# The order of the steps on five queues of a decoder block, written anew

## The chip, the cores and the metric

The kernel runs on one core of one Trainium2 chip. The metric is the device time in microseconds (us), the median of three runs. The profile comes from one execution of its own. Engines in the profile: PE is TensorE, PEld its weight loads, DVE is VectorE, ACT is ScalarE, POOL is GpSimd, SPq the sync queue, which here issues all transfers.

## The reference

One decoder block for 32 batches of 256 tokens with 256 features, in float32. Each of the three parts works on a LayerNorm of x and is added to x:

```
x = x + attn(layernorm(x))          # a: 8 heads of 128, one shared K and V, causal softmax, Wo
x = x + xattn(layernorm(x), ctx)    # b: 16 heads of 16 on a context of 256 tokens;
                                    #    scores get two bias tensors (one of 32x16x256x256) and a padding mask
x = x + ffn(layernorm(x))           # c: shared expert 0 and 8 experts of 256, relu squared,
                                    #    gate: top 2 of 8, sigmoid, normalized
```

## The kernel before

Matmuls are done in float16 pairs (a high and a low part of each operand, three products), so each tile has a `hi` and a `lo` that engines other than TensorE make. Each of the five queues (sync, GpSimd, ScalarE, VectorE, TensorE) has a list of steps, written out by hand in `ORDERS`. An entry `b_s:5@4` is step `b_s` for head 5 of the batch 4 iterations back. `iterations` walks each list 32 + 6 times and emits the steps whose batch exists. So the three parts run at once on different batches: in the loop part a is some two batches ahead of part c. A queue works strictly in its list's order; steps wait for each other through semaphores that count, and the same name on several engines is one step's share on each.

The steps that matter here, with their lines:

- `b_load:p` (sync, L363 to L368) loads the bias of a pair of heads, 512 KB, into one of four slots, once VectorE has read the slot (`b_s` of head 2p+1). `b_pT:j` (sync, L421) transposes head j's probabilities by DMA. `b_store_q`, `b_store_k` write q and k to DRAM (L388, L381), `b_stack_q`, `b_stack_k` read them back stacked, 8 loads each (L413, L402). `b_s:0` on TensorE waits for all 16.
- `b_s:j`: scores on TensorE (L1088, two matmuls, which wait until VectorE has done head j-1), bias and maximum on VectorE (L828), exponential on ScalarE (L662, L664, which waits for VectorE's `b_p` of head j-1). `b_p:j`: probabilities, high part on ScalarE (L672), low part on VectorE (L835). `b_pv:j` on TensorE (L1102). `b_comb:j` (GpSimd, L520) adds the mask to the bias.
- `b_mask` (VectorE, L814) makes the mask of a batch; `b_ln`, `b_T`, `b_q`, `b_kv`, `b_o`, `b_wo` are LayerNorm, its transposition, the projections and the output of part b.
- `a_wo` is part a's output projection, 48 matmuls; `a_kv` and `a_q:r` its projections (TensorE's `a_q:0` waits for VectorE's `a_kv`, L758), `a_s:h`, `a_pt:h`, `a_pv:h` scores, transposition and values of head h.
- `c_ln`, `c_T` (L992, then ScalarE L582 and VectorE L743) give part c its input. `c_gate` on TensorE are 16 small matmuls; on VectorE `c_gate:0` to `c_gate:12` are 13 steps on 8 or 16 columns, of which `c_gate:4` (L890) waits for ScalarE's exponential (L684), `c_gate:5` casts (L893), `c_gate:6` makes masks (L898). `c_f1:e` is expert e's first matmul (TensorE L965), relu (ScalarE L690) and square (GpSimd L534), `c_sq:e` the high part of the square (ScalarE L695), `c_lo:e` the low part (GpSimd L541). `c_f2:e` is the second matmul and, on VectorE, the sum into `acc` (L936); TensorE's `c_f2:e` waits for VectorE's `c_f2:e-1`, and VectorE's `c_f2:1` for the last gate step.
- `w_split:n` (ScalarE and VectorE) splits a piece of the weights, in the first batch alone.

TensorE's waits in two of these steps read:

```
            def b_s(b, j):
                if j == 0:
                    pe.wait_ge(b_qst_ok, after(b, STACK, STACK))
                    pe.wait_ge(b_kst_ok, after(b, STACK, STACK))
                pe.wait_ge(b_t_ok, after(b, BH, j))
...
            def c_f2(b, e):
                pe.wait_ge(c_h_ok, after(b, NX, e + 1))
                if e == 0:
                    pe.wait_ge(c_gd, after(b, GATE_STEPS, 1))
                else:
                    pe.wait_ge(c_a_ok, after(b, NX, e))
```

Of the kernel before, what the change touches and what calls it, by code (L numbers as in the profile page):

```python
# [66 lines left out]
def order(text):  # L67
# [9 lines left out]
        b_pT:11@5 b_load:5@5 b_pT:13@5 b_load:7@5 b_store_q:0@4 b_pT:14@5 b_store_k:0@4 b_pT:15@5 b_stack_q:0@4  # L77
        b_stack_k:0@4 a_T:0@3 b_load:6@5 b_load:0@4 b_pT:0@4 b_load:1@4 b_pT:1@4 c_f2:8@6 b_pT:2@4 b_pT:3@4
        b_pT:4@4 b_load:2@4 b_pT:5@4 b_pT:6@4 b_mask:0@4 b_split_q:0@3 b_load:3@4 a_ln:0@3 b_pT:8@4 b_pT:7@4
        b_pT:9@4 b_pT:10@4 b_load:4@4 b_pT:12@4""",  # L80
    gpsimd="""
        b_comb:9@5 b_comb:10@5 b_comb:11@5 c_lo:4@6 c_f1:5@6 c_lo:5@6 c_f1:6@6 b_comb:12@5 a_ln:0@3 b_ln:0@4
        b_comb:13@5 b_comb:14@5 a_kv:0@3 b_comb:15@5 c_lo:6@6 a_q:0@3 b_split_q:0@4 c_f1:7@6 c_lo:7@6
        b_split_k:0@4 a_q:1@3 b_comb:0@4 a_q:2@3 c_f1:8@6 c_lo:8@6 a_q:3@3 b_comb:1@4 b_kv:0@3 b_comb:2@4
        c_ln:0@5 b_comb:3@4 b_v:0@4 b_comb:4@4 b_comb:5@4 c_f1:0@5 c_lo:0@5 b_comb:6@4 c_f1:1@5 b_comb:7@4
        c_lo:1@5 c_f1:2@5 c_lo:2@5 b_res:0@4 c_f1:3@5 c_lo:3@5 b_comb:8@4 c_f1:4@5""",
    scalar="""
        a_n:3@2 a_pt:2@2 a_pv:1@2 a_s:6@2 a_n:4@2 b_s:0@3 c_ln:0@4 b_p:0@3 a_pt:3@2 c_T:0@4 a_pv:2@2 b_s:1@3
        b_p:1@3 a_n:5@2 a_pt:4@2 b_s:2@3 c_f1:0@4 b_p:2@3 c_gate:0@4 c_sq:0@4 a_s:7@2 c_f1:1@4 b_s:3@3 a_pv:3@2
        w_split:9@2 b_p:3@3 c_f1:2@4 a_pt:5@2 c_sq:1@4 b_s:4@3 c_f1:3@4 b_p:4@3 w_split:10@2 c_sq:2@4  # L90
        w_split:11@2 a_n:6@2 c_f1:4@4 b_s:5@3 b_p:5@3 a_pv:4@2 c_sq:3@4 a_pt:6@2 b_s:6@3 b_p:6@3 c_f1:5@4
        a_n:7@2 b_s:7@3 a_pv:5@2 b_p:7@3 c_sq:4@4 w_split:12@2 c_f1:6@4 b_s:8@3 a_pv:6@2 a_pt:7@2 b_p:8@3
        c_sq:5@4 w_split:13@2 w_split:14@2 w_split:15@2 a_pv:7@2 b_s:9@3 b_p:9@3 c_f1:7@4 b_s:10@3 b_p:10@3
# [1135 lines left out]
```

## Time and profile before

| | |
|---|---|
| median of 3 runs | 2400.63 us (2398.98 to 2402.5) |
| the profiled execution | 2400.63 us, its span 2398.8 us |
| mean granted TensorE clock | 0.954 |
| busy shares | PE 89%, ACT 87%, DVE 83%, POOL 74% |
| chain that ended last | PE 48%, DVE 21%, issue 14%, ACT 13% |
| transfers | 367 MB, 153 GB/s, 70.7% of the 16 DMA engines' time |

Busy shares are of the span. The chain is followed back from the last instruction; "issue" in it, and as the releaser of a wait, is time for which no engine's work is the cause that the profile shows. The clock is the share of full speed (2.4 GHz) that TensorE was granted; 0.50 is 1.2 GHz. The span from batch to batch is called an interval below, from one start of `b_wo` on TensorE to the next.

### The profile page before, as it was taken

The numbers are of one execution on the slowest core, as the hardware profiler recorded it, in microseconds if no ns is written. First come the engines' busy times: TensorE is split into PE (matmuls) and PEld (weight loads), VectorE is DVE, ScalarE is ACT, GpSimd is POOL, SyncE is SP. The second block draws the span as 40 slices with busy tenths as digits, with TensorE's granted clock in tenths as the row PEclk, the third lists the DMA queues.
The fourth block names the chain that finished last, engine by engine and source line by source line (L and its number), as shares of the span: only waits on it lengthen the run. The fifth ranks groups of instructions, "written<-read, shape, count | busy, mean of one in ns | idle before, by whom it ended". The sixth has DMA issues, their size and how long they took to land.

```text
span 2398.8 us, 73036 instructions
## 1 busy us (share of the span) xinstructions
PE 2130.8 (89%) x24128; PEld 1855.2 (77%) x24128; DVE 1987.0 (83%) x6672; ACT 2079.4 (87%) x6065; POOL 1786.7 (74%) x1899
## 2 busy tenths in 40 slices
PE   4679999999999999998999999999999988999876
PEld 3468888888877878887778888888888877788755
DVE  5478889888888888888888888899888888888763
ACT  5589999988988999998999999999998889899862
POOL 2448788877877877877877878787778777777773
PEclk9789999999999999999999999999999999999987
DMA  4377766768767788877867777677678678878760
GB/s 148 113 173 155 168 146 162 171 153 160 159 155 142 173 157 158 162 155 138 169 155 164 161 157 163 145 174 160 161 163 156 150 147 158 162 160 157 142 145 22
DMA packets 711784, 367.16 MB, mean 153 GB/s; under 512 B 561392, under 2 KB 659952, under 8 KB 711408
## 3 DMA queue, kind: packets, MB, share of 16 engines
q1 hardware_dynamic: 711408, 362.50, 70.7%
q8 instruction: 193, 3.16, 0.6%
q14 instruction: 183, 1.50, 0.2%
HBM read 202.98 MB, written 25.17 MB: 95 GB/s over the span
## 4 chain that ended last, share of the span: by engine, by line
PE 48%; DVE 21%; issue 14%; ACT 13%; POOL 2%; DMA 2%; SPq 0%; DVEq 0%; ACTq 0%; POOLq 0%
PE ps_a_misc L965 13%; PE ps_c_hidden L965 10%; PE ps_c_out L965 9%; PE ps_a_scores L1025 4%; DVE b_neg_scores L828 3%; DVE g_mask L898 2%; PE ps_b_misc L1102 2%; PE ps_b_scores L1088 2%; ACT ps_b_probs L664 2%; PE ps_a_misc L1044 2%; DVE b_probs_hi_lo L835 2%; ACT ps_b_probs L662 2%; ACT b_probs_hi_lo L672 2%; DVE g_weights L920 1%; DVE g_sum L913 1%
## 5 line engine op out<-in xcount | busy, mean ns | idle before, releaser
L520 POOL TENSOR_TENSOR bias<-bias,b_mask 128x512 f32<-128x512 f32 x512 | 646.4, 1274 | 7.2 <-DMA bias<-in_bias 7.0
L835 DVE TENSOR_TENSOR b_probs_hi_lo<-ps_b_probs,b_probs_hi_lo 128x512 f16<-128x512 f32 x512 | 351.8, 687 | 128.9 <-ACT b_probs_hi_lo L672 127.3
L828 DVE CUSTOM_DVE_ANT_0 b_neg_scores<-ps_b_scores,bias 128x256 f32<-128x256 f32 x1024 | 389.3, 417 | 72.0 <-PE ps_b_scores L1088 60.4
L534 POOL TENSOR_TENSOR c_hidden<-c_relu 128x512 f32<-128x512 f32 x288 | 299.8, 1041 | 152.7 <-ACT c_relu L690 138.0
L541 POOL TENSOR_TENSOR c_hidden_lo<-c_hidden,c_hidden_hi 128x512 f16<-128x512 f32 x288 | 334.2, 1160 | 59.8 <-issue 39.4
L662 ACT ACTIVATE ps_b_probs<-b_neg_scores,b_neg_max 128x256 f32<-128x256 f32 x512 | 245.4, 479 | 144.0 <-DVE b_probs_hi_lo L835 108.7
L965 PE MATMUL ps_c_hidden<-c_xT_hi,w_hi 128*128 128x256 f16 x1152 | 325.1, 282 | 40.1 <-ACT c_relu L690 40.0
L965 PE MATMUL ps_c_out<-w_hi,c_hidden_hi 128*128 128x256 f16 x1152 | 316.1, 274 | 29.0 <-DVE acc L936 28.9
L965 PE MATMUL ps_c_hidden<-c_xT_lo,w_hi 128*128 128x256 f16 x1152 | 324.0, 281 | 0.0
L965 PE MATMUL ps_c_hidden<-c_xT_hi,w_lo 128*128 128x256 f16 x1152 | 323.6, 281 | 0.0
L965 PE MATMUL ps_c_out<-w_hi,c_hidden_lo 128*128 128x256 f16 x1152 | 316.3, 275 | 0.0
L965 PE MATMUL ps_c_out<-w_lo,c_hidden_hi 128*128 128x256 f16 x1152 | 316.2, 274 | 0.0
L672 ACT ACTIVATE b_probs_hi_lo<-ps_b_probs 128x512 f16<-128x512 f32 x512 | 303.1, 592 | 8.4
L936 DVE SCALAR_TENSOR_TENSOR acc<-ps_c_out,g_weights,acc 128x256 f32<-128x256 f32 x512 | 218.6, 468 | 29.6 <-PE ps_c_out L965 29.6
L664 ACT ACTIVATE ps_b_probs<-b_neg_scores,b_neg_max 128x256 f32<-128x256 f32 x512 | 239.9, 469 | 0.0
L1102 PE MATMUL ps_b_misc<-b_v_hi,b_probsT_hi_lo 128*128 128x16 f16 x4096 | 217.1, 170 | 5.6 <-DMA b_probsT_hi_lo<-b_probs_hi_lo 5.5
L1102 PEld LDWEIGHTS ps_b_misc<-b_v_hi,b_probsT_hi_lo 128*128 128x128 f16 x4096 | 203.2, 96 | 11.5 <-DMA b_probsT_hi_lo<-b_probs_hi_lo 7.0
L478 POOL TENSOR_TENSOR a_qT_lo<-a_qT,a_qT_hi 128x512 f16<-128x512 f32 x128 | 148.8, 1162 | 78.6 <-ACT a_qT_hi L601 74.7
L690 ACT ACTIVATE c_relu<-ps_c_hidden 128x512 f32<-128x512 f32 x288 | 169.9, 590 | 31.3 <-PE ps_c_hidden L965 27.7
L1102 PE MATMUL ps_b_misc<-b_v_lo,b_probsT_hi_lo 128*128 128x16 f16 x2048 | 194.1, 169 | 0.0
L695 ACT ACTIVATE c_hidden_hi<-c_relu 128x512 f16<-128x512 f32 x288 | 181.9, 632 | 5.8 <-PE ps_c_out L965 5.8
L965 PE MATMUL ps_a_misc<-a_xT_hi,w_hi 128*128 128x256 f16 x576 | 159.4, 277 | 13.3 <-DVE a_v_lo L758 8.8
(194 smaller groups left out, 7752.5 us busy)
## 6 DMA issues: line engine op xcount, KB each, us to landing
bias<-in_bias SPq DMA_DIRECT2D x256, 512.0 KB, 4.1
q_stack<-qk_scratch SPq DMA_DIRECT2D x256, 64.0 KB, 3.6
x_ln<-in_x SPq DMA_DIRECT2D x32, 256.0 KB, 3.1
ctxT<-in_ctx SPq DMA_DIRECT2D x32, 256.0 KB, 2.8
x<-in_x SPq DMA_DIRECT2D x32, 256.0 KB, 4.0
qk_scratch<-b_qT_hi_lo SPq DMA_DIRECT2D x32, 256.0 KB, 5.5
qk_scratch<-b_kT_hi_lo SPq DMA_DIRECT2D x32, 256.0 KB, 4.2
k_stack_even<-qk_scratch SPq DMA_DIRECT2D x128, 64.0 KB, 2.9
```

The source lines that it names most:

```text
L520: gp.tensor_tensor(part, part, b_mask[:, :], ALU.add).then_inc(b_c_ok, 1)
L534: gp.tensor_tensor(c_h[:, :], c_r[:, e % 2, :], c_r[:, e % 2, :], ALU.mult).then_inc(c_sq_ok, 1)
L541: gp.tensor_tensor(c_hl[:, u, :], c_h[:, :], c_hh[:, u, :], ALU.subtract).then_inc(c_h_ok, 1)
L662: act.activation(ps_bp[:, 0:T], b_t[:, u, 0, :], ACT.Exp, bias=b_mx[:, u, 0:1], scale=-1.0, accum_out=b_sum[:, 0, j:j + 1])
L664: act.activation(ps_bp[:, T:2 * T], b_t[:, u, 1, :], ACT.Exp, bias=b_mx[:, u, 1:2], scale=-1.0, accum_out=b_sum[:, 1, j:j + 1]).then_inc(b ...
L672: act.activation(b_p2[:, j % DEPTH, :, 0, :], ps_bp[:, :].rearrange("p (c t) -> p c t", c=CT), ACT.Copy).then_inc(b_ph_ok, 1)
L695: act.activation(c_hh[:, e % 2, :], c_r[:, e % 2, :], ACT.Square).then_inc(c_hh_ok, 1)
L828: last = dve.tensor_tensor_reduce(out=b_t[:, u, c, :], in0=ps_bs[:, c * T:(c + 1) * T], in1=bias[:, slot, at:at + T], scale=-2.0, scalar=3 ...
L835: dve.tensor_tensor(b_p2[:, j % DEPTH, :, 1, :], ps_bp[:, :].rearrange("p (c t) -> p c t", c=CT), b_p2[:, j % DEPTH, :, 0, :], ALU.subtrac ...
L936: last = dve.scalar_tensor_tensor(out=acc[:, c, :], in0=ps_c2[:, c * D:(c + 1) * D], scalar=g_we[:, c, e - 1:e], in1=acc[:, c, :], op0=ALU ...
L965: last = pe.matmul(out, stat(s, k), mov(m, k), start=(k == 0 and n == 0), stop=(k == chunks - 1 and n == len(parts) - 1))
L1102: last = pe.matmul(ps_bm[:, at:at + BD], b_pT[:, u, c, part, s, :], v[:, s, j * BD:(j + 1) * BD], start=(s == 0 and n == 0), stop=(s == CT ...
```

## The change

All five lists in `ORDERS` are replaced. Each has the same steps as before, once each, so the instructions, their shapes and their number stay; what changes is the place of a step in its queue and with it what it waits behind. Where a list begins is of no weight by itself (a list that starts one step later has its lags written differently), only the order in the endless round counts. `w_split` entries count for the first batch alone. The lines of the old and the new lists that the text speaks of:

```diff
     sync="""
-        b_pT:11@5 b_load:5@5 b_pT:13@5 b_load:7@5 b_store_q:0@4 b_pT:14@5 b_store_k:0@4 b_pT:15@5 b_stack_q:0@4
-        b_stack_k:0@4 a_T:0@3 b_load:6@5 b_load:0@4 b_pT:0@4 b_load:1@4 b_pT:1@4 c_f2:8@6 b_pT:2@4 b_pT:3@4
-        b_pT:4@4 b_load:2@4 b_pT:5@4 b_pT:6@4 b_mask:0@4 b_split_q:0@3 b_load:3@4 a_ln:0@3 b_pT:8@4 b_pT:7@4
-        b_pT:9@4 b_pT:10@4 b_load:4@4 b_pT:12@4""",
+        b_load:7@5 b_store_q:0@4 b_pT:14@5 b_mask:0@4 b_store_k:0@4 b_pT:15@5 b_stack_q:0@4 b_stack_k:0@4
+        c_f2:8@6 b_load:0@4 b_pT:0@4 b_pT:1@4 b_load:1@4 a_ln:0@3 a_T:0@3 b_pT:2@4 b_pT:3@4 b_pT:4@4 b_load:3@4
+        b_load:2@4 b_pT:5@4 b_pT:7@4 b_pT:6@4 b_load:4@4 b_pT:8@4 b_split_q:0@3 b_load:5@4 b_pT:9@4 b_pT:10@4
+        b_pT:11@4 b_load:6@4 b_pT:12@4 b_pT:13@4""",
     gpsimd="""
...
-        c_ln:0@5 b_comb:3@4 b_v:0@4 b_comb:4@4 b_comb:5@4 c_f1:0@5 c_lo:0@5 b_comb:6@4 c_f1:1@5 b_comb:7@4
-        c_lo:1@5 c_f1:2@5 c_lo:2@5 b_res:0@4 c_f1:3@5 c_lo:3@5 b_comb:8@4 c_f1:4@5""",
+        b_v:0@4 b_comb:5@4 a_q:3@3 b_comb:6@4 c_ln:0@5 b_res:0@4 c_f1:0@5 c_lo:0@5 c_f1:1@5 c_lo:1@5 b_kv:0@3
+        c_f1:2@5 c_lo:2@5 b_comb:7@4 c_f1:3@5 b_comb:8@4 c_lo:3@5 b_comb:9@4 c_f1:4@5 c_lo:4@5 c_f1:5@5 c_lo:5@5
+        b_comb:10@4 b_comb:11@4 c_f1:6@5 b_comb:12@4 a_ln:0@2 c_lo:6@5 b_comb:13@4 b_ln:0@3 b_comb:14@4
...
     scalar="""
-        a_n:3@2 a_pt:2@2 a_pv:1@2 a_s:6@2 a_n:4@2 b_s:0@3 c_ln:0@4 b_p:0@3 a_pt:3@2 c_T:0@4 a_pv:2@2 b_s:1@3
-        b_p:1@3 a_n:5@2 a_pt:4@2 b_s:2@3 c_f1:0@4 b_p:2@3 c_gate:0@4 c_sq:0@4 a_s:7@2 c_f1:1@4 b_s:3@3 a_pv:3@2
...
+        a_n:2@2 a_q:3@2 a_n:3@2 a_pv:0@2 a_s:4@2 a_s:5@2 a_pt:2@2 a_pv:1@2 w_split:10@2 a_n:4@2 b_s:0@3 c_ln:0@4
+        b_p:0@3 a_pt:3@2 c_T:0@4 a_n:5@2 b_s:1@3 a_pv:2@2 b_p:1@3 w_split:11@2 c_f1:0@4 a_pt:4@2 c_sq:0@4
+        b_s:2@3 c_f1:1@4 b_p:2@3 c_gate:0@4 c_sq:1@4 a_s:6@2 c_f1:2@4 b_s:3@3 a_pv:3@2 b_p:3@3 c_sq:2@4 c_f1:3@4
+        a_s:7@2 b_s:4@3 a_pt:5@2 b_p:4@3 c_f1:4@4 a_n:6@2 b_s:5@3 a_pv:4@2 b_p:5@3 c_sq:3@4 a_pt:6@2 b_s:6@3
...
     vector="""
...
-        a_pt:7@3 b_p:8@4 b_s:10@4 a_pv:7@3 b_p:9@4 a_ln:0@2 a_ln:1@2 c_f2:4@5 b_s:11@4 w_split:3@2 b_p:10@4
-        a_wo:0@3 b_ln:0@3 b_ln:1@3 b_s:12@4 b_p:11@4 a_T:0@2 c_f2:5@5 b_s:13@4 b_p:12@4 a_kv:0@2 b_T:0@3 a_q:0@2
-        b_s:14@4 w_split:4@2 b_p:13@4 b_s:15@4 a_q:1@2 b_p:14@4 a_s:0@2 b_mask:0@3 b_p:15@4 a_s:1@2 a_r:0@2
...
-        c_T:0@4 b_s:2@3 a_pv:2@2 b_p:1@3 c_gate:0@4 b_s:3@3 a_r:6@2 c_gate:1@4 w_split:8@2 a_pt:4@2 c_gate:2@4
-        b_p:2@3 c_gate:3@4 c_gate:4@4 b_s:4@3 c_gate:5@4 a_pv:3@2 c_gate:6@4 b_p:3@3 c_gate:7@4 b_s:5@3
-        c_gate:8@4 w_split:9@2 c_f2:0@4 c_gate:9@4 b_p:4@3 c_gate:10@4 a_pt:5@2 c_gate:11@4 b_s:6@3 c_gate:12@4
-        b_p:5@3 c_f2:1@4 w_split:10@2 a_r:7@2 w_split:11@2 b_s:7@3 a_pv:4@2 b_p:6@3 a_pt:6@2 c_f2:2@4""",
+        a_pv:1@3 b_s:1@4 a_s:6@3 w_split:10@3 b_p:0@4 c_T:0@5 a_pt:3@3 b_s:2@4 a_pv:2@3 b_p:1@4 b_s:3@4
+        c_gate:0@5 c_gate:1@5 c_gate:2@5 a_s:7@3 c_gate:3@5 c_gate:4@5 c_gate:5@5 b_p:2@4 c_gate:6@5 a_pt:4@3
+        w_split:11@3 c_gate:7@5 b_s:4@4 c_f2:0@5 c_gate:8@5 c_gate:9@5 b_p:3@4 c_gate:10@5 c_gate:11@5 a_r:6@3
+        a_pv:3@3 b_s:5@4 c_gate:12@5 c_f2:1@5 a_r:7@3 a_pt:5@3 b_p:4@4 b_s:6@4 a_pv:4@3 b_p:5@4 c_f2:2@5
...
+        w_split:3@2 b_p:10@4 a_wo:0@3 b_s:11@4 b_ln:0@3 b_s:12@4 b_ln:1@3 b_p:11@4 c_f2:5@5 b_s:13@4 a_T:0@2
+        b_p:12@4 b_T:0@3 b_mask:0@3 w_split:4@2 a_kv:0@2 b_s:14@4 w_split:5@2 b_p:13@4 a_q:0@2 w_split:6@2
...
     tensor="""
-        a_s:5@3 c_f2:8@6 a_s:6@3 b_wo:0@5 a_pt:2@3 a_pv:1@3 a_s:7@3 b_s:0@4 b_s:1@4 a_pt:3@3 a_pv:2@3 c_T:0@5
-        b_s:2@4 a_pt:4@3 c_gate:0@5 b_s:3@4 c_f1:0@5 a_pv:3@3 b_s:4@4 c_f1:1@5 a_pt:5@3 b_pv:0@4 c_f1:2@5
-        c_f2:0@5 b_s:5@4 c_f1:3@5 a_pv:4@3 b_pv:1@4 c_f1:4@5 b_s:6@4 b_pv:2@4 c_f2:1@5 a_pt:6@3 c_f1:5@5 b_s:7@4
-        b_pv:3@4 c_f2:2@5 b_s:8@4 a_pv:5@3 c_f1:6@5 c_f2:3@5 a_pt:7@3 b_s:9@4 a_pv:6@3 c_f1:7@5 b_pv:4@4
...
-        b_pv:7@4 b_s:13@4 a_kv:0@2 b_pv:8@4 b_T:0@3 b_s:14@4 b_pv:9@4 a_q:0@2 b_q:0@3 a_q:1@2 b_s:15@4 b_pv:10@4
...
+        b_s:1@4 a_pt:3@3 c_T:0@5 b_s:2@4 a_pv:2@3 a_s:7@3 c_f1:0@5 a_pt:4@3 b_s:3@4 c_gate:0@5 c_f1:1@5 a_pv:3@3
+        b_s:4@4 b_pv:0@4 c_f1:2@5 c_f2:0@5 c_f1:3@5 b_s:5@4 a_pt:5@3 c_f2:1@5 c_f1:4@5 b_s:6@4 a_pv:4@3 c_f2:2@5
+        b_pv:1@4 b_pv:2@4 a_pt:6@3 c_f1:5@5 b_s:7@4 a_pv:5@3 b_pv:3@4 c_f2:3@5 b_s:8@4 c_f1:6@5 a_pt:7@3 b_s:9@4
...
+        a_T:0@2 c_f1:8@5 b_pv:6@4 b_s:13@4 b_pv:7@4 c_f2:6@5 b_s:14@4 b_T:0@3 a_kv:0@2 b_pv:8@4 b_q:0@3 a_q:0@2
...
+        c_f2:8@5 a_s:5@2 b_wo:0@4 a_pt:2@2 a_pv:1@2 a_s:6@2 b_s:0@3""",
...
```

## Rows read from the trace of the kernel before

**Rows 1.** Page, part 1: busy us (share of the span) xinstructions.
```profile
PE 2130.8 (89%) x24128; PEld 1855.2 (77%) x24128; DVE 1987.0 (83%) x6672; ACT 2079.4 (87%) x6065; POOL 1786.7 (74%) x1899
```

**Rows 2.** The write of x2, L862: count, ns min/median/max, first and last start.
```profile
L862 DVE SCALAR_TENSOR_TENSOR x<-ps_b_misc,x_bo x32: 691/692/694, 169.8 to 2352.9; 128x512 f32<-128x512 f32 x32
```

**Rows 3.** Two intervals: us; busy PE, PEld, DVE, ACT, POOL; PEclk, DMA share.
```profile
1579.40:1648.30 68.90, 63.63 (x756) 56.62 (x754) 61.45 (x209) 64.11 (x191) 55.60 (x60) 1.00 0.73 162
1858.40:1930.30 71.90, 67.45 (x756) 59.01 (x754) 61.51 (x209) 64.44 (x190) 54.50 (x59) 0.93 0.78 155
```

**Rows 4.** Waits: engine, line, releaser: us in total, times, longest.
```profile
PE ps_c_hidden L965 <- ACT c_relu L690: 40.0, 83, 0.9
...
PE ps_b_scores L1088 <- issue: 33.5, 22, 2.8
...
PE ps_c_out L965 <- DVE acc L936: 28.9, 35, 2.9
```

**Rows 5.** Timeline, sync queue, slow interval: start us, us of issuing.
```profile
1907.94 0.57 SPq L368 DMA_DIRECT2D bias<-in_bias  x1
...
1913.97 0.57 SPq L368 DMA_DIRECT2D bias<-in_bias  x1
...
1915.92 0.61 SPq L368 DMA_DIRECT2D bias<-in_bias  x1
...
1922.04 4.83 SPq L413 DMA_DIRECT2D q_stack<-qk_scratch  x8
...
1928.80 1.86 SPq L402 DMA_DIRECT2D k_stack_odd<-qk_scratch  x4
```

**Rows 6.** Timeline, TensorE behind those issues: start, us, [idle before <-releaser].
```profile
1935.90 0.59 PE L1088 MATMUL ps_b_scores<-k_stack_even,q_stack 128*128 128x256 f16 x2 [2.76 <-issue]
```

**Rows 7.** Stretches of 6 us of the slow interval, columns as in rows 3.
```profile
1867.00:1873.00 6.00, 5.71 (x41) 3.86 (x40) 4.99 (x20) 4.84 (x16) 1.04 (x1) 0.50 0.57 135
1909.00:1915.00 6.00, 5.78 (x71) 5.16 (x70) 4.14 (x13) 5.97 (x18) 4.70 (x5) 1.00 1.10 158
...
1921.00:1927.00 6.00, 6.00 (x98) 5.56 (x96) 5.82 (x22) 5.91 (x20) 4.64 (x5) 1.00 1.26 181
```

**Rows 8.** Timeline of TensorE in the short interval.
```profile
1579.83 0.27 PE L965 MATMUL ps_b_misc<-w_lo,b_oT_hi 128*128 128x256 f16 x1
1579.94 0.27 PE L965 MATMUL ps_b_misc<-w_hi,b_oT_lo 128*128 128x256 f16 x1
...
1583.70 0.39 PE L1088 MATMUL ps_b_scores<-k_stack_odd,q_stack 128*128 128x256 f16 x2 [1.30 <-DVE b_neg_max L828]
...
1585.81 0.66 PE L992 MATMUL ps_c_hidden<-constants,c_xn 128*128 128x128 f32 x4 [0.54 <-ACT c_xn L573]
...
1587.57 0.30 PE L1032 MATMUL ps_a_probsT<-constants,a_probs 128*128 128x128 f32 x1 [0.89 <-DVE a_probsT_lo L766]
```

**Rows 9.** The same engine, later in that interval.
```profile
1628.02 0.28 PE L965 MATMUL ps_a_misc<-a_xT_hi,w_hi 128*128 128x256 f16 x1 [0.23 <-DVE a_v_lo L758]
```

**Rows 10.** Timeline of VectorE, two of the gate's steps.
```profile
1592.91 1.02 DVE L890 TENSOR_SCALAR g_exp<-g_exp 128x16 f32<-128x16 f32 x1
...
1595.59 1.79 DVE L898 TENSOR_SCALAR g_mask<-constants,g_idx_f 128x8 f32<-128x8 f32 x2
```

**Rows 11.** Timeline of GpSimd beside them.
```profile
1592.74 1.16 POOL L541 TENSOR_TENSOR c_hidden_lo<-c_hidden,c_hidden_hi 128x512 f16<-128x512 f32 x1
```

**Rows 12.** Line 893: count, ns min/median/max, first and last start.
```profile
L893 DVE CAST g_idx_f<-g_idx x32: 171/623/635, 184.5 to 2365.3; 128x4 f32<-128x4 uint32 x32
```

**Rows 13.** Line 898, the same columns.
```profile
L898 DVE TENSOR_SCALAR g_mask<-constants,g_idx_f x64: 219/828/1322, 185.5 to 2366.4; 128x8 f32<-128x8 f32 x64
```

**Rows 14.** Timeline of VectorE behind a_wo.
```profile
1622.85 0.42 DVE L828 CUSTOM_DVE_ANT_0 b_neg_scores<-ps_b_scores,bias 128x256 f32<-128x256 f32 x1
```

**Rows 15.** The same engine, b_mask.
```profile
1635.32 2.22 DVE L814 SCALAR_TENSOR_TENSOR b_mask<-key_padding,half_mask 128x256 f32<-128x256 uint8 x2
```

**Rows 16.** Line 814: count, ns min/median/max, first and last start.
```profile
L814 DVE SCALAR_TENSOR_TENSOR b_mask<-key_padding,half_mask x64: 414/925/1377, 95.1 to 2277.2; 128x256 f32<-128x256 uint8 x64
```

More of the change, by code:

```diff
@@ L81 @@
+        c_f2:8@6 b_load:0@4 b_pT:0@4 b_pT:1@4 b_load:1@4 a_ln:0@3 a_T:0@3 b_pT:2@4 b_pT:3@4 b_pT:4@4 b_load:3@4
+        b_load:2@4 b_pT:5@4 b_pT:7@4 b_pT:6@4 b_load:4@4 b_pT:8@4 b_split_q:0@3 b_load:5@4 b_pT:9@4 b_pT:10@4
+        b_pT:11@4 b_load:6@4 b_pT:12@4 b_pT:13@4""",
     gpsimd="""
-        b_comb:9@5 b_comb:10@5 b_comb:11@5 c_lo:4@6 c_f1:5@6 c_lo:5@6 c_f1:6@6 b_comb:12@5 a_ln:0@3 b_ln:0@4
-        b_comb:13@5 b_comb:14@5 a_kv:0@3 b_comb:15@5 c_lo:6@6 a_q:0@3 b_split_q:0@4 c_f1:7@6 c_lo:7@6
@@ L84 @@
-        b_split_k:0@4 a_q:1@3 b_comb:0@4 a_q:2@3 c_f1:8@6 c_lo:8@6 a_q:3@3 b_comb:1@4 b_kv:0@3 b_comb:2@4
-        c_ln:0@5 b_comb:3@4 b_v:0@4 b_comb:4@4 b_comb:5@4 c_f1:0@5 c_lo:0@5 b_comb:6@4 c_f1:1@5 b_comb:7@4
-        c_lo:1@5 c_f1:2@5 c_lo:2@5 b_res:0@4 c_f1:3@5 c_lo:3@5 b_comb:8@4 c_f1:4@5""",
-    scalar="""
-        a_n:3@2 a_pt:2@2 a_pv:1@2 a_s:6@2 a_n:4@2 b_s:0@3 c_ln:0@4 b_p:0@3 a_pt:3@2 c_T:0@4 a_pv:2@2 b_s:1@3
-        b_p:1@3 a_n:5@2 a_pt:4@2 b_s:2@3 c_f1:0@4 b_p:2@3 c_gate:0@4 c_sq:0@4 a_s:7@2 c_f1:1@4 b_s:3@3 a_pv:3@2
[L90 to L93, printed above, removed]
-        c_sq:6@4 w_split:3@0 b_s:11@3 a_ln:0@1 b_p:11@3 c_f1:8@4 a_T:0@1 b_s:12@3 b_ln:0@2 w_split:4@1 b_p:12@3
-        a_kv:0@1 b_T:0@2 c_sq:7@4 b_s:13@3 b_p:13@3 w_split:5@1 a_q:0@1 b_q:0@2 b_s:14@3 b_p:14@3 b_kv:0@2
-        b_s:15@3 w_split:6@1 b_p:15@3 a_q:1@1 a_s:0@1 a_n:0@1 a_s:1@1 a_pt:0@1 a_q:2@1 c_sq:8@4 w_split:7@1
-        a_s:2@1 a_q:3@1 a_n:1@1 a_s:3@1 a_pt:1@1 a_pv:0@1 b_o:0@3 w_split:8@1 a_n:2@1 a_s:4@1 a_s:5@1 b_v:0@2""",
@@ new lines @@
+    tensor="""
+        b_s:1@4 a_pt:3@3 c_T:0@5 b_s:2@4 a_pv:2@3 a_s:7@3 c_f1:0@5 a_pt:4@3 b_s:3@4 c_gate:0@5 c_f1:1@5 a_pv:3@3
+        b_s:4@4 b_pv:0@4 c_f1:2@5 c_f2:0@5 c_f1:3@5 b_s:5@4 a_pt:5@3 c_f2:1@5 c_f1:4@5 b_s:6@4 a_pv:4@3 c_f2:2@5
+        b_pv:1@4 b_pv:2@4 a_pt:6@3 c_f1:5@5 b_s:7@4 a_pv:5@3 b_pv:3@4 c_f2:3@5 b_s:8@4 c_f1:6@5 a_pt:7@3 b_s:9@4
+        a_pv:6@3 b_pv:4@4 c_f2:4@5 a_pv:7@3 c_f1:7@5 b_s:10@4 a_wo:0@3 b_s:11@4 b_pv:5@4 c_f2:5@5 b_s:12@4
+        a_T:0@2 c_f1:8@5 b_pv:6@4 b_s:13@4 b_pv:7@4 c_f2:6@5 b_s:14@4 b_T:0@3 a_kv:0@2 b_pv:8@4 b_q:0@3 a_q:0@2
+        b_pv:9@4 b_s:15@4 b_kv:0@3 a_q:1@2 b_pv:10@4 b_pv:11@4 a_s:0@2 b_kv:1@3 b_pv:12@4 a_s:1@2 b_pv:13@4
+        a_q:2@2 a_pt:0@2 a_s:2@2 c_f2:7@5 a_s:3@2 a_pt:1@2 b_pv:14@4 b_pv:15@4 a_q:3@2 b_o:0@4 a_s:4@2 a_pv:0@2
+        c_f2:8@5 a_s:5@2 b_wo:0@4 a_pt:2@2 a_pv:1@2 a_s:6@2 b_s:0@3""",
```

21 lines of the change are left out of this document (14 added, 7 removed).

## The prediction

> **What bounds the kernel now.** I read the page's busy shares first [rows 1]: TensorE 89%, ScalarE 87%, VectorE 83%, GpSimd 74%. No engine is full, so the order in which the engines meet matters. The writes of x2 show the rhythm: 32 of them, 169.8 to 2352.9 us [rows 2], (2352.9 - 169.8) / 31 = 70.4 us from batch to batch. With about 170 us ahead of the first and 46 us behind the last, nearly the whole time is 31 such intervals, so 1 us more in each is 31 us.
>
> Two intervals side by side [rows 3]: 68.9 us with TensorE's granted clock at 1.00, and 71.9 us with 0.93. The short one is what the orders alone allow; the mean lies 1.5 us above it. The list of waits says where that comes from [rows 4]: ahead of the scores of an even head (L1088, `b_s`) TensorE waits 33.5 us in 22 times, released by "issue", which means nothing on an engine: a transfer. 33.5 / 31 = 1.1 us per interval. It is the first head, `b_s:0`, waiting for the 16 loads of `q_stack` and `k_stack`. The remaining 0.4 us is the clock: one such wait is 2.76 us long [rows 6], and in the slow interval a stretch of 6 us behind it is granted 0.50, that is 1.2 in place of 2.4 GHz [rows 7].
>
> In the undisturbed interval TensorE's gaps lie close together [rows 8]: 1.30 us before `b_s:1`, 0.54 before `c_T`, 0.89 before `a_pt:4`, and 0.23 before `a_q:0` [rows 9]. The waits for c_relu add 40.0 / 31 = 1.3 us per interval (before `c_f1:1`, `c_f1:2`, `c_f1:4`), those for acc 28.9 us in 35 times, 0.8 each (before `c_f2:2`) [rows 4]. Matmuls take 0.27 us and start 0.11 apart [rows 8], so each gap costs its length plus 0.16 us of overlap.
>
> **The change.** The instructions, their number and their sizes stay. Only their order within each queue changes. So I costed it by walking through the new order from `b_wo` on, each step starting when its queue and its inputs allow, with durations from the undisturbed interval. Three places matter.
>
> (1) *The bias loads, 512 KB each.* In the old sync order `b_load:4` stands behind `b_pT:10`, `b_load:5` behind `b_pT:11`, `b_load:6` behind the stack loads. In a disturbed interval these loads leave at 1907.9, 1914.0 and 1915.9, and the 16 stack loads follow from 1922.0 on [rows 5]. There the DMA engines are at 1.10 to 1.26 of their share, against 0.57 earlier in the interval [rows 7] and 0.78 over all of it [rows 3]. In the new order `b_load:4` stands behind `b_pT:6` and leaves when `b_s:9` is done, by my walk some 11 us earlier; `b_load:5` goes ahead of `b_pT:9`, some 7 us earlier; `b_load:6` leaves behind `b_pT:11`, ahead of the stacks. Only `b_load:7` is still next to them, so one load of the two or three is out of the crowded stretch. The new neighbours in the queue: `b_load:3` waits for `b_s:7` and holds back `b_pT:5`, and `b_load:5` waits for `b_s:11` and holds back `b_pT:9`; their readers `b_pv:5` and `b_pv:9` stand behind `a_wo`, 48 matmuls of 0.11 us, 5.3 us, so I cost that at nothing (without that cover it would be some 2 us). `b_mask`'s small load ahead of `b_store_k` waits for work that is done earlier in the new order: nothing. The distance from `b_p:15` and `b_kv` to `b_s:0` stays, within 0.2 us of TensorE's work, so the stacks have as long as now, 13.9 us from the first issue to `b_s:0` where it is late (1922.0 to 1935.9) [rows 5, 6]. Bounds: 0 (the issues of the 16 loads, 8.6 us from 1922.04 to 1930.66, set the landing whatever else flows) to 1.5 us per interval. I take -1.3, the 1.1 us of waits and half of the clock's 0.4, because with one and the same order the wait came in 22 of 31 intervals and reached 2.76 us, which traffic explains better than a fixed chain of issues.
>
> (2) *From `b_wo` to `c_f2:2`.* The new tensor order has `a_pv:2` and `a_s:7` behind `c_T` and puts `c_f1:0` ahead of `c_gate`, so the wait for LayerNorm's transposed result is filled. Walked through, the waits up to `b_s:5` fall from 4.9 us (seven: 1.30, 0.54, 0.89, two of c_relu with 0.75, two small ones with 0.3, and 7 x 0.16) to 3.3 us (1.39 at `b_s:1`, 0.33 at `a_pt:3`, 1.19 at `c_T`, 0.36 at `c_f1:0`): -1.6. But the gate's 13 small VectorE steps now stand closer. `c_gate:4` needs ScalarE's exponential, which is now queued behind `c_f1:1` and `b_p:2`, and VectorE's `b_p:2` and `b_s:4` stand behind `c_gate:5` and `c_gate:7`. The gate's steps are dear: 1.02 us for 16 elements (L890), 1.79 for two masks (L898) [rows 10], 0.62 in the median for a cast (L893) [rows 12]. They end when the GpSimd instruction beside them ends: L890 at 1592.91 + 1.02 = 1593.93 [rows 10], GpSimd's L541 at 1592.74 + 1.16 = 1593.90 [rows 11]; the shortest cast of the 32 takes 171 ns [rows 12], the shortest mask 219 [rows 13]. So their price is set by where they fall in GpSimd's stream: in my walk `b_s:4` ends at 17.8 us behind `b_wo`'s start where TensorE wants `b_s:5` at 16.9, 0.9 us lost; then 0.5 before `b_s:6` and 1.1 before `c_f2:2`, which needs `c_f2:1` and so the gate's end. That is 2.5 us against 1.7 now (0.6 before `c_f1:4`, 0.8 before `c_f2:2`, 2 x 0.16): +0.8. `c_lo:3` comes 0.3 us late for `c_f2:3` because `c_sq:3` stands behind `b_p:5`: +0.3. Sum: -0.5. If the cast loses its race for the port, the sum is +0.7 to +2.0 instead.
>
> (3) *Behind `a_wo`.* The new vector order puts `b_s:11` ahead of `b_ln:0` and `b_s:12` ahead of `b_ln:1`, each two instructions of 0.42 us [rows 14]; `b_T` waits 0.55 us. `b_mask` (2.22 us [rows 15]) moves from behind `a_s:0` to between `b_T` and `a_kv`, whose result TensorE needs for `a_q:0`. Its two instructions take 414 to 1377 ns each [rows 16], so `a_q:0` loses 0.2 to 1.2 us, with 0.15 before `b_q`. Together 0.9 to 1.9, against 0.4 now: +0.5 to +1.5, I take +0.9.
>
> Head and tail: each engine's steps move by few places against each other and the depth of six iterations stays; the pieces of the weights are split earlier, but the last (`w_split:15`) within two places of where it was. I take 0, bounds -5 and +5 us.
>
> Sum per interval: -1.3 - 0.5 + 0.9 = -0.9 us, times 31 = -28 us. The profiled execution took 2400.63 us at a span of 2398.8 and is also the median of the three runs, so the forecast is 2373 us.
>
> **The port.** The gate's rows [rows 10, 11] show an engine that waits for the whole instruction of the other. The Trainium skill, page "SBUF — State Buffer", section "Who interferes with whom", says that VectorE and GpSimd share one pair of ports as an exclusive lock, and that the second one to ask is blocked fully until the first is through. By that rule the trace agrees for L890, L893 and L898. It would let the closer-packed gate steps run into the three GpSimd instructions of `b_kv`, which the new order puts between `c_lo:1` and `c_f1:2`, and thus speaks for the first rival.
>
> **Rivals.**
> *The gate chain becomes the bound (slower).* Place: VectorE from `c_gate:4` to `c_f2:1`. `c_gate:4` ends about when GpSimd's `c_f1:1` does; then `c_gate:5` and GpSimd's `c_lo:1` both become ready within 0.1 us. If GpSimd starts first, the cast waits 1.2 us, `c_gate:6` falls behind two more instructions, and `b_s:5` loses 1.9 to 2.8 us, not 0.9. Then (2) is +0.7 to +2.0 instead of -0.5, 1.35 in the middle, and the sum is -1.3 + 1.35 + 0.9 = +1.0: 2400.6 + 31 = 2431 us, 2410 to 2450. It decides from a wait at `b_s:5` of some 1.8 us on. For it: the median cast, 623 ns, is one that waited [rows 12]. Against it: some found the port free [rows 12, 13].
> *The loads don't matter.* The sixteen issues set the landing, `b_s:0` keeps its 1.1 us: -0.1 - 0.5 + 0.9 = +0.3, 2410 us. With the first rival as well: +2.2, 2469 us. For it: the issues alone fill 8.6 of the 13.9 us. Against it: the intervals without any wait.
> *The change does nothing.* Gains and losses at TensorE's gaps cancel, with the loads' help small: 2400 us.
>
> **How the numbers follow.** Chances: forecast 0.40; gate chain 0.33; loads don't matter 0.12; both 0.10; nothing 0.05. Low end: loads worth the full 1.5, (3) at its lower bound: -1.5 in the interval, and a few us of the head: 2345. High end: the gate chain at its upper bound, 2450, which leaves out the case of both. Runs of this kernel differ by 0.15%, so 0.2% (4.8 us) is about what can be told from no change. Faster: 0.40, plus 0.06 from the weaker forms of the other cases; same 0.10; slower 0.44.
>
> **What would show it.** Right: the wait of `b_s:0` by "issue" falls from 33.5 us to under 8; the DMA share in the 18 us ahead of the stacks' landing falls to about 1.0; TensorE's gap before `a_pt:4` is gone, a new one of 0.5 to 1 us stands before an odd head's scores (`b_s:5`) in the FFN part; a gap before `b_T`. Wrong: gaps over 1.8 us at `b_s:5` or before `c_f2:2`, a granted clock that falls a second time in the interval, or the stack's wait unchanged.

## The result, and the profile after

The new orders took 2489.93 us (median of four executions, 2487.29 to 2491.76) against 2400.86 us before, also of four: ratio 1.037, 95% interval 1.0352 to 1.0389. One further execution of the new orders took 4171.51 us at a granted clock of 1.00 and is left out as a slow one; nothing on record says why. The prediction, 2373 us with a range of 2345 to 2450, had the wrong sign and missed the range. It had put 0.44 on slower.

The page after, part 1, busy us and share of the span [rows 1]; and the write of x2 [rows 2]. Lines of the kernel after are one higher than before (L862 is L863); in the runs e5 to e7 and e9 to e14 the vector list is a line shorter, so that they have the numbers of before again.

```profile
PE 2161.2 (87%) x24128; PEld 1852.2 (75%) x24128; DVE 1964.2 (79%) x6672; ACT 2070.0 (83%) x6065; POOL 1785.0 (72%) x1899
```

```profile
L863 DVE SCALAR_TENSOR_TENSOR x<-ps_b_misc,x_bo x32: 681/692/694, 166.9 to 2438.5; 128x512 f32<-128x512 f32 x32
```

(2438.5 - 166.9) / 31 = 73.3 us per interval against 70.4: 2.9 us more, in 31 intervals 88.5 us. Head and tail are 3 and 4 us shorter after, so that the spans of the two profiled executions differ by 2480.6 - 2398.8 = 81.8 us. (The profiled execution after took 2482.43 us, 7.5 us less than the median.) The list of waits of TensorE after, with us in total, times, longest:

```profile
PE ps_c_out L966 <- DVE acc L937: 90.2, 66, 2.8
PE ps_b_scores L1089 <- DVE b_neg_max L829: 74.4, 105, 2.2
PE ps_c_hidden L993 <- ACT c_xn L574: 35.8, 32, 4.9
...
PE ps_b_scores L1089 <- issue: 23.8, 27, 2.0
PE ps_b_misc L1103 <- DMA b_probsT_hi_lo<-b_probs_hi_lo: 12.4, 18, 1.2
PE ps_a_misc L1045 <- DVE a_oT_lo L774: 9.3, 6, 4.9
...
PE ps_a_probsT L1033 <- DVE a_probsT_lo L767: 7.0, 31, 1.3
...
PE ps_c_hidden L966 <- ACT c_relu L691: 1.2, 3, 0.7
```

The rows of the kernel before that answer to these and are not in [rows 4]:

```profile
PE ps_b_scores L1088 <- DVE b_neg_max L828: 41.7, 39, 2.3
...
PE ps_a_probsT L1032 <- DVE a_probsT_lo L766: 24.6, 63, 2.5
...
PE ps_c_hidden L992 <- ACT c_xn L573: 16.7, 23, 4.9
...
PE ps_b_misc L1102 <- DMA b_probsT_hi_lo<-b_probs_hi_lo: 5.5, 7, 1.2
...
PE ps_a_misc L1044 <- DVE a_oT_lo L773: 1.7, 3, 0.7
```

Read as differences: `c_f2`'s wait for acc +61.3 us, odd and even scores' wait for VectorE +32.7, `c_T` +19.1, transposed probabilities +6.9, a_oT_lo +7.6; c_relu -38.8, `a_pt` -17.6, the stack loads (issue) -9.7. These eight make +61.5 us; the whole lists, of 259.8 us before and 313.0 after, differ by +53.2. The mean granted clock fell from 0.954 to 0.946. A share of the span (1 - clock) is time that TensorE lost to the lower level: 0.046 x 2398.8 = 110 us before, 0.054 x 2480.6 = 134 after, +24 us. The two add to 77 us, where the span grew by 81.8. About 5 us are left: the rounding of the two clocks is worth up to 2.4 us, and the lists hold 15 gaps more after (359 against 344), each with the prediction's 0.16 us of overlap, another 2.4. So no third cause is needed.

One interval, from `b_wo` on (1637.99 us). The columns are those of [rows 3]: the interval, the gap before `c_f2:2`, the 3.4 us behind it, and what follows.

```profile
1637.99:1709.90 71.91, 64.87 (x735) 56.17 (x733) 59.06 (x202) 62.22 (x186) 53.28 (x59) 0.95 0.73 153
1662.30:1664.80 2.50, 0.18 (x3) 0.00 (x0) 2.37 (x6) 0.77 (x3) 1.40 (x2) 1.00 0.02 4
1665.80:1669.20 3.40, 3.40 (x40) 2.74 (x38) 2.54 (x9) 3.25 (x11) 0.75 (x1) 0.51 0.52 82
1669.20:1672.00 2.80, 2.80 (x38) 2.56 (x37) 1.98 (x7) 2.45 (x8) 2.72 (x4) 0.99 0.00 0
```

TensorE stands nearly still for 2.5 us while VectorE works through, and just behind it the clock is at half (0.51) and back at 0.99 after 3.4 us. Such a stretch is not in every interval. Counted from the clock in the two traces, 22 of the 31 intervals before had one behind `b_s:0`, none had one at `c_f2:2`. After, 21 have the one behind `b_s:0`, 23 have one behind `c_f2:2`, 13 have both. The same place on the four engines (start, us):

```profile
1661.59 0.39 PE L1089 MATMUL ps_b_scores<-k_stack_even,q_stack 128*128 128x256 f16 x2 [0.44 <-DVE b_neg_max L829]
...
1664.88 0.27 PE L966 MATMUL ps_c_out<-w_hi,c_hidden_hi 128*128 128x256 f16 x1 [2.40 <-DVE acc L937]
...
1666.09 0.42 PE L966 MATMUL ps_c_out<-w_lo,c_hidden_hi 128*128 128x256 f16 x1
```

```profile
1661.46 2.27 DVE L921 TENSOR_SCALAR g_weights<-g_w,g_inv 128x8 f32<-128x8 f32 x2
1663.86 0.88 DVE L937 SCALAR_TENSOR_TENSOR acc<-ps_c_out,g_weights,acc 128x256 f32<-128x256 f32 x2
...
1665.18 0.68 DVE L836 TENSOR_TENSOR b_probs_hi_lo<-ps_b_probs,b_probs_hi_lo 128x512 f16<-128x512 f32 x1
```

```profile
1661.43 1.04 POOL L535 TENSOR_TENSOR c_hidden<-c_relu 128x512 f32<-128x512 f32 x1
1662.43 1.27 POOL L521 TENSOR_TENSOR bias<-bias,b_mask 128x512 f32<-128x512 f32 x1
1668.45 1.16 POOL L542 TENSOR_TENSOR c_hidden_lo<-c_hidden,c_hidden_hi 128x512 f16<-128x512 f32 x1 [4.75 <-issue]
```

```profile
1665.95 0.48 ACT L663 ACTIVATE ps_b_probs<-b_neg_scores,b_neg_max 128x256 f32<-128x256 f32 x1 [2.89 <-DVE b_probs_hi_lo L836]
```

The last gate step, `c_gate:12` (L921, two instructions on 8 columns), takes 2.27 us: the first starts beside GpSimd's `c_f1:3`, the second beside `b_comb:8`, and the pair ends at 1663.73 where `b_comb:8` ends, at 1663.70. Then `c_f2:1` (L937) runs until 1664.74, and TensorE's `c_f2:2` starts at 1664.88. A second way out of the same place: VectorE's `b_p:4` (L836) stands behind these steps, ScalarE's `b_s:5` waits 2.89 us for it, `c_sq:3` stands behind that, and GpSimd's `c_lo:3`, which TensorE needs for `c_f2:3`, is idle for 4.75 us. The experiments had to tell which way sets the time, or whether VectorE's queue as a whole does.

By the prediction's marks: `b_s:0`'s wait fell only to 23.8 us (under 8 wanted); the DMA share in the 18 us ahead of `b_s:0` is 0.97 in the mean of 30 intervals after, but it was 0.98 before already; the gap before `a_pt:4` is gone, and `b_s:5` waits 0.50 us, both as forecast; `c_f2:2` waits in every interval, 2.40 us in the median (1.8 was the mark for wrong), and in 23 of 31 the clock falls there.

### The profile page after: what moved, and what is told of

Read it like the earlier page. It is cut to its first block, busy times and chain, and to the rows that moved or that the text cites. A ratio compares the mean times of both kernels' runs of the same rounds, so it can differ in the third digit from the quotient of the medians.

```text
span 2480.6 us, 73034 instructions
## 1 busy us (share of the span) xinstructions
PE 2161.2 (87%) x24128; PEld 1852.2 (75%) x24128; DVE 1964.2 (79%) x6672; ACT 2070.0 (83%) x6065; POOL 1785.0 (72%) x1899
## 4 chain that ended last, share of the span: by engine, by line
PE 52%; DVE 17%; issue 12%; ACT 12%; DMA 4%; SPq 2%; POOL 1%; DVEq 0%; ACTq 0%; POOLq 0%
PE ps_a_misc L966 12%; PE ps_c_hidden L966 11%; PE ps_c_out L966 10%; DMA b_probsT_hi_lo<-b_probs_hi_lo 4%; PE ps_a_scores L1026 4%; PE ps_b_misc L1103 3%; DVE g_weights L921 3%; PE ps_a_misc L1045 3%; PE ps_b_scores L1089 3%; ACT ps_b_probs L665 2%; DVE b_neg_scores L829 2%; ACT ps_b_probs L663 2%; PE ps_b_misc L966 2%; ACT b_probs_hi_lo L673 1%; DVE g_mask L899 1%
## 5 line engine op out<-in xcount | busy, mean ns | idle before, releaser
L836 DVE TENSOR_TENSOR b_probs_hi_lo<-ps_b_probs,b_probs_hi_lo 128x512 f16<-128x512 f32 x512 | 349.0, 682 | 126.9 <-ACT b_probs_hi_lo L673 119.1
L966 PE MATMUL ps_c_out<-w_hi,c_hidden_hi 128*128 128x256 f16 x1152 | 321.8, 279 | 92.6 <-DVE acc L937 90.2
L966 PE MATMUL ps_c_out<-w_hi,c_hidden_lo 128*128 128x256 f16 x1152 | 324.4, 282 | 0.0
L966 PE MATMUL ps_c_out<-w_lo,c_hidden_hi 128*128 128x256 f16 x1152 | 323.5, 281 | 0.0
L937 DVE SCALAR_TENSOR_TENSOR acc<-ps_c_out,g_weights,acc 128x256 f32<-128x256 f32 x512 | 222.1, 475 | 34.7 <-PE ps_c_out L966 30.0
L966 PEld LDWEIGHTS ps_c_out<-w_hi,c_hidden_hi 128*128 128x128 f16 x1152 | 114.5, 99 | 122.2 <-issue 104.3
```

The source lines that it names most:

```text
L836: dve.tensor_tensor(b_p2[:, j % DEPTH, :, 1, :], ps_bp[:, :].rearrange("p (c t) -> p c t", c=CT), b_p2[:, j % DEPTH, :, 0, :], ALU.subtrac ...
L937: last = dve.scalar_tensor_tensor(out=acc[:, c, :], in0=ps_c2[:, c * D:(c + 1) * D], scalar=g_we[:, c, e - 1:e], in1=acc[:, c, :], op0=ALU ...
L966: last = pe.matmul(out, stat(s, k), mov(m, k), start=(k == 0 and n == 0), stop=(k == chunks - 1 and n == len(parts) - 1))
```

## The experiments

Edits are shown as the places in the lists that changed. None leaves work out. Each ratio is to the kernel before, with its 95% interval.

**1 and 2: fill the gap; take GpSimd away from the gate's last step.** Both on the new orders.

```diff
     tensor (e1)
-        ... a_pv:4 c_f2:2 b_pv:1 b_pv:2 a_pt:6 c_f1:5 b_s:7 ...
+        ... a_pv:4 b_pv:1 b_pv:2 c_f1:5 c_f2:2 a_pt:6 b_s:7 ...
     gpsimd (e2)
-        ... c_f1:3 b_comb:8 c_lo:3 b_comb:9 ...
+        ... c_f1:3 c_lo:3 b_comb:8 b_comb:9 ...
```

> The new orders, but on TensorE c_f2:2 now stands behind b_pv:1, b_pv:2 and c_f1:5 (it stood ahead of them). Theory (TensorE asks for c_f2:2 some 2.4 us before VectorE can have finished the gate and c_f2:1, and the idle stretch also brings a second stretch at half clock): about 2.0 us of matmuls fill the gap, it falls from 2.40 to some 0.3 us, the second half-clock stretch (3.4 us, some 1.0 us of lost time) goes, together 2.9 us in each of 31 intervals, so 2490 - 90 = 2400 us, 2395 to 2425. Rival A (VectorE as a whole is the bound, the gap at c_f2:2 only shows it): the wait moves to another step of TensorE, 2480 to 2495 us. Rival B (the gap is the whole loss, the clock is granted half as often as before): 2490 - 31 x 1.9 = 2431 us.

Measured: 2491.28 us, 1.0387 (1.0362 to 1.0413). Nothing gained: my theory fell, and the wait moved, as rival A has it. TensorE's waits with the fill:

```profile
PE ps_a_misc L1045 <- DVE a_oT_lo L774: 37.9, 37, 4.9
...
PE ps_c_out L966 <- DVE acc L937: 32.1, 66, 2.1
PE ps_c_out L966 <- POOL c_hidden_lo L542: 27.5, 32, 2.2
```

The wait for acc fell by 58.1 us (90.2 to 32.1), but 28.6 us came back at `a_pv:5` (a_oT_lo, 9.3 to 37.9) and 26.1 at `c_f2:3` (c_hidden_lo, 1.4 to 27.5): both hang on the second way out, the late `b_p:4` (ScalarE's `a_pv:4`, too, stands behind the `b_s:5` that waits for it). The clock stayed at 0.947.

> The new orders, but on GpSimd b_comb:8 stands behind c_lo:3 (it stood ahead of it, beside VectorE's last gate step, whose two instructions on 8 columns take 2.27 us there against 1.25 in the old orders). Theory (that step waits out one GpSimd instruction after the other, and its length is passed on to c_f2:1 and c_f2:2): the step falls to about 1.2 us, the gap before c_f2:2 from 2.40 to 1.3, 31 x 1.1 = 34 us less, 2456 us; 2425 if the second half-clock stretch goes with it. Rival A (VectorE's queue, not the gate's last step, sets c_f2:1): under 10 us less, 2480 to 2492. Rival C (the step is long for a reason of its own): the step stays above 2 us and the time at 2490.

Measured: 2450.17 us, 1.0209 (1.0192 to 1.0226): -40 us, near the theory's 2456. Count, ns min/median/max of L921, after and in this run:

```profile
L921 DVE TENSOR_SCALAR g_weights<-g_w,g_inv x64: 217/1052/1310, 187.0 to 2458.7; 128x8 f32<-128x8 f32 x64
```

```profile
L921 DVE TENSOR_SCALAR g_weights<-g_w,g_inv x64: 217/226/1048, 186.5 to 2424.2; 128x8 f32<-128x8 f32 x64
```

One of the two instructions now finds GpSimd silent (median 226 ns) and the other still waits `c_f1:3` out. The wait for acc fell from 90.2 to 54.2 us (`c_f2:2` now waits 1.31 us in the median), the one for c_hidden_lo rose from 1.4 to 13.7, and the clock rose to 0.956: no interval has a half-clock stretch at `c_f2:2` any more. So the step's length is the GpSimd instruction beside it, and it is passed on. Here a rule of the Trainium skill can be checked, page "SBUF — State Buffer", section "Who interferes with whom": VectorE's instructions in a two-port mode (a tensor_scalar can enter one) contend with GpSimd, and so do those with two SBUF inputs when GpSimd's instruction reads SBUF; those with at most one SBUF input outside such a mode do not. The traces agree: L921 waits; L937, with one input in PSUM, takes 475 ns in the median after and 474 before.

**3, 4 and 8: the sync order.**

```diff
     e3: the kernel before, the new sync list      e4: the new orders, the old sync list
     sync (e8, on the kernel before)
-        b_pT:11@5 b_load:5@5 b_pT:13@5 ... a_T:0@3 b_load:6@5 b_load:0@4 ...
-        ... b_pT:8@4 b_pT:7@4 b_pT:9@4 b_pT:10@4 b_load:4@4 b_pT:12@4
+        b_pT:11@5 b_load:6@5 b_pT:13@5 ... a_T:0@3 b_load:0@4 ...
+        ... b_pT:8@4 b_pT:7@4 b_load:4@4 b_pT:9@4 b_load:5@4 b_pT:10@4 b_pT:12@4
```

> The kernel before with the new sync order alone. The prediction's term (1) says that bias loads that leave earlier free the DMA engines for the stack loads: 1.3 us per interval, 2400.6 - 40 = 2360 us, and b_s:0 waits for issue under 8 us in all. What the changed kernel's trace suggests (its wait is 23.8 us in 27 times, against 33.5 in 22): 0.3 us per interval, 2391 us. Rival (the 16 issues set the landing): 2400 us.

Measured: 2630.46 us, 1.0953 (1.0935 to 1.0972), far from each of the three numbers expected. The whole list can't test the loads, because it moves something else too. Sync queue (L353 is `a_ln`'s load, L421 the transposes), GpSimd (L527 is `b_res`) and TensorE (`b_pv:2`) in one interval:

```profile
1688.23 0.33 SPq L353 DMA_DIRECT2D x<-in_x  x1
1688.61 0.42 SPq L359 DMA_DIRECT2D x_ln<-in_x  x1
1689.13 4.20 SPq L421 DMA_TRANSPOSE b_probsT_hi_lo<-b_probs_hi_lo  x3
```

```profile
1686.80 1.41 POOL L527 TENSOR_TENSOR x_bo<-x,bo 128x256 f32<-128x256 f32 x2
```

```profile
1693.05 0.20 PE L1102 MATMUL ps_b_misc<-b_v_hi,b_probsT_hi_lo 128*128 128x16 f16 x1 [6.74 <-DMA b_probsT_hi_lo<-b_probs_hi_lo]
```

The new list has `a_ln` ahead of `b_pT:2`. `a_ln` waits for `b_res`, which the old GpSimd order reaches late (1688.21), so three transposes leave at 1689.13 and TensorE waits 6.7 us. In the new orders `b_res` stands early, and TensorE's longest wait for a transpose is 1.2 us.

> The changed kernel with the old sync order: the other four lists stay new. The prediction's term (1): 2490 + 40 = 2530 us. From the changed kernel's trace: 0.3 us per interval, 2499 us. Rival (the loads' places are worth nothing): 2490 us. If it is faster than 2480, the new sync order itself is part of the loss (b_load:3 and b_load:5 hold back transposes behind them, b_pv:15 waits more often than before).

Measured: 2776.18 us, 1.155 (1.1523 to 1.1578). The mirror image: GpSimd waits 324.1 us in 34 times (up to 12.1) for a bias load, and TensorE 241.1 us in 31 times (up to 9.3) for GpSimd's a_qT_lo behind it. None of the three numbers that I had written came near; the two runs say only that the sync list and the others fit together.

> The kernel before, in which only three bias loads leave earlier in the sync order: b_load:4 behind b_pT:7, b_load:5 behind b_pT:9, b_load:6 behind b_pT:11. No other step changes its place. The prediction's term (1): the wait of b_s:0 for the stack loads falls from 33.5 us to under 8 us in all, 2400 - 35 = 2365 us, 2355 to 2385. Rival (the sixteen issues set the landing, what else flows does not matter): the wait stays at 30 to 35 us, 2400 us. Rival (the loads, now ahead of transposes in the queue, hold these back): waits of b_pv for the transposes rise above the 5.5 us of before, 2405 to 2440.

Measured: 2395.23 us, 0.9977 (0.9963 to 0.9992). This is the test of term (1) alone:

```profile
PE ps_b_scores L1088 <- issue: 26.9, 18, 3.6
```

The wait fell from 33.5 us to 26.9, not to 8, and the gain is 0.23% of the time by the ratio, 5.5 us or 0.2 us per interval (3.5 us by the medians). TensorE's waits for transposes did not become a bound.

**5, 6 and 7: both ways out of the gate.** On the new orders.

```diff
     vector (e5, e6, e7)
-        ... b_s:5 c_gate:12 c_f2:1 a_r:7 a_pt:5 b_p:4 b_s:6 ...
+        ... b_s:5 a_pt:5 b_p:4 c_gate:12 c_f2:1 a_r:7 b_s:6 ...
     tensor (e6, e7): as in e1          gpsimd (e7): as in e2
```

> The new orders, but on VectorE a_pt:5 and b_p:4 stand ahead of c_gate:12 and c_f2:1 (they stood behind). What the first four runs left: theory V (the loss runs along VectorE's last gate step, then b_p:4 behind it, ScalarE's b_s:5 which waits for b_p:4, c_sq:3 behind b_s:5, GpSimd's c_lo:3, TensorE's c_f2:3; and in parallel c_f2:1, TensorE's c_f2:2). By V this move takes c_lo:3 some 3 us ahead (it then ends at about 28.4 us behind b_wo's start, not at 31.6), but puts c_f2:1 about 0.3 us later, so TensorE's gap before c_f2:2 stays at 2.3 to 2.7 us and the time at 2480 to 2500 us. Rival T (only the distance from the gate to c_f2:2 matters): +0.3 us per interval, 2500 us. Rival S (ScalarE's idle 2.9 us before b_s:5 is what the interval lacks): 2490 - 31 x 2 = 2430 us.

Measured: 2487.89 us, 1.0355 (1.0331 to 1.038), as by theory V, and within 0.5% of rival T's 2500. ScalarE's 2.9 us of idle time was no loss by itself (rival S is out), and `c_f2:2`'s gap stayed, at 2.53 us in the median.

> The move of the run before and, on TensorE, c_f2:2 behind b_pv:1, b_pv:2 and c_f1:5, as in the first fill. Theory V: both ways out of the gate are now covered, gaps at c_f2:2 about 0.3 to 0.6, at a_pv:5 and c_f2:3 none (0.94 and 0.81 in the first fill), and no second half-clock stretch: -1.9 - 0.98, 2490 - 31 x 2.9 = 2400 us, 2385 to 2425. Rival T: as without this fill, the gap only moves, 2490 us.

Measured: 2417.15 us, 1.0061 (1.0038 to 1.0084). Two moves that gave 2 us and -1 us alone give 73 us together, and rival T (2490 us) is out. TensorE's wait for acc:

```profile
PE ps_c_out L965 <- DVE acc L936: 36.5, 67, 2.2
```

It fell by 53.7 us (from 90.2), a_oT_lo's went back from 37.9 to 14.8, c_hidden_lo's from 27.5 to 1.1, and the clock rose to 0.958, 102 us lost instead of 134.

> All three moves: a_pt:5 and b_p:4 ahead of the last gate step, c_f2:2 behind b_pv:1, b_pv:2 and c_f1:5, and GpSimd's b_comb:8 behind c_lo:3. Theory V: the last gate step takes 0.5 to 1.2 us instead of 2.3, so the rest of the gap at c_f2:2 goes: 5 to 25 us less than without this third move, 2370 to 2395 us. Rival: what sets the interval is then elsewhere (the gaps at b_s:1, c_T and b_s:0), no gain over the two moves.

Measured: 2401.49 us, 1.0000 (0.998 to 1.002): three moves of steps bring the new orders back to the time of before, 16 us below the run above. That is the theory's 5 to 25 us, though the time lies above its 2370 to 2395.

```profile
PE ps_c_out L965 <- DVE acc L936: 16.4, 36, 2.1
```

```profile
L920 DVE TENSOR_SCALAR g_weights<-g_w,g_inv x64: 219/223/230, 189.9 to 2381.8; 128x8 f32<-128x8 f32 x64
```

All 64 instructions of the last gate step now take 219 to 230 ns.

**9 to 13: the other places, on the version of e7.**

```diff
     vector (e9, e13)
-        ... b_T:0 b_mask:0 w_split:4 a_kv:0 b_s:14 ...
+        ... b_T:0 w_split:4 a_kv:0 b_mask:0 b_s:14 ...
     tensor (e10, e12, e13)
-        ... a_pt:3 c_T:0 b_s:2 a_pv:2 a_s:7 ...
+        ... a_pt:3 a_pv:2 c_T:0 b_s:2 a_s:7 ...
     vector (e11, e12; e14 moves b_s:4 alone)
-        ... b_p:2 c_gate:6 a_pt:4 c_gate:7 b_s:4 c_f2:0 c_gate:8 c_gate:9 b_p:3 c_gate:10 ... a_pv:3 b_s:5 a_pt:5 ...
+        ... b_p:2 b_s:4 c_gate:6 a_pt:4 c_gate:7 c_f2:0 c_gate:8 c_gate:9 b_p:3 b_s:5 c_gate:10 ... a_pv:3 a_pt:5 ...
```

> Base: the version with all three moves (2401 us). On VectorE b_mask stands behind a_kv, no longer ahead of it. The prediction's term (3) says that b_mask's place ahead of a_kv costs a_q:0 0.2 to 1.2 us per interval: 2401 - 31 x 0.8 = 2376 us, 2364 to 2395. From the traces (TensorE's gap before a_q:0 is 0.24 us here against 0.23 before the change, so it costs only this remainder and 0.16 of overlap, 0.4 us at most): 2389 us if nothing else takes it back, 2401 if it only moves.

Measured: 2390.01 us, 0.995 (0.9933 to 0.9968), 11 us less, the size that the trace gave (2389) and not the prediction's. But the way is another: `a_q:0`'s gap went, and more than it came back behind it (`b_s:15`, `b_kv:1`, `a_pt:0` each start 0.2 us later in the mean against the step ahead of them, mostly in delays too short for the list of waits). What fell besides are two waits for transfers, `b_s:0`'s for the stack from 28.2 to 17.9 us and those for transposes from 15.7 to 8.2, and the clock's loss, from 0.045 x 2405.1 = 108 us to 0.037 x 2388.2 = 88. The profiled span fell by 2405.1 - 2388.2 = 16.9 us. Why moving `b_mask` helps the transfers is open.

> Same base. On TensorE a_pv:2 stands ahead of c_T, as in the old order, and fills a part of the 0.91 us gap there (0.28 in the old orders, where a_pv:2 and a_s:7 stood ahead). Theory (TensorE's own path sets the time from b_s:0 to b_s:3, where VectorE waits 1.59 us for it): 0.5 us of matmuls, 31 x 0.5 = 15 us less, 2385 us, a little more if the half clock behind c_T (a_pv:2, a_s:7 and c_f1:0 take 0.9 us longer than at full clock) goes. Rival (VectorE sets the time further on and gives it back): 2401 us.

Measured: 2377.68 us, 0.9902 (0.9879 to 0.9925): 24 us less, faster than both kernels. TensorE's waits for LayerNorm (first row `c_T`'s):

```profile
PE ps_c_hidden L992 <- ACT c_xn L573: 20.4, 29, 4.9
...
PE ps_c_hidden L965 <- DVE c_xT_lo L743: 11.4, 16, 1.4
```

In e7 they were 34.4 and 3.7 us: 14.0 less and 7.7 more, 6 us in all. The larger part is the clock, 0.968 against 0.955 in the profiled executions, 76 us lost instead of 108. (The other executions of e7 were granted 0.952 to 0.965, those of e10 0.965 to 0.968.)

> Same base. On VectorE b_s:4 stands right behind b_p:2, ahead of c_gate:6, and b_s:5 right behind b_p:3, ahead of c_gate:10; these are what TensorE's b_s:5 and b_s:6 wait for (0.50 and 0.44 us). Theory V (from c_gate:4 to c_f2:1 VectorE is never idle, 16.4 to 26.7 us behind b_wo's start, and its sum of work there sets c_f2:2): the two gaps go and come back before c_f2:2, gain under 0.3 us per interval, 2392 to 2401 us. Rival T (these two waits are losses by themselves, the prediction's way to count them): 31 x 1.26 = 39 us less, 2362 us.

Measured: 2459.51 us, 1.0242 (1.022 to 1.0264), 58 us slower; both theories fell. The two waits did go, but TensorE waited 1.85 us at `c_f2:1`, which none had foreseen, because `c_gate:7` took 1.85 us instead of 0.44.

> Same base, the moves of the two runs before together. Theory V: their gains add, 2377 to 2388 us. If it is under 2395 it beats both kernels.

Measured: 2423.85 us, 1.009 (1.0071 to 1.011). The expected sum of gains failed with e11's: the move of `a_pv:2` gives 36 us here (24 alone), the loss of the other stays.

> Base: the version with the three moves (2401 us). b_mask behind a_kv on VectorE and a_pv:2 ahead of c_T on TensorE, which alone gave 2390 and 2378 us. The two places lie some 40 us apart in the interval, and both alone were bound by TensorE's own path: gains add, 2401 - 11 - 24 = 2366 us, 2360 to 2375, below both kernels. Rival (one and the same slack): 2378 us.

Measured: 2378.11 us, 0.9912 (0.9888 to 0.9936). The gains don't add; the rival's time held. Its reason, one and the same slack, is not shown: in the trace `b_mask`'s gains are there again (`b_s:0`'s wait 18.9 us against 28.6 in e10, TensorE's for a_kv 1.3 against 8.8), and other delays take them back. `a_pv:2` alone is the simplest version below both kernels.

**14 and 15: the price of a gate step, and the early ask alone.**

> Same base. On VectorE only b_s:4 stands ahead of c_gate:6; b_s:5 keeps its place. With both moved c_gate:7 took 1.85 us instead of 0.44 and TensorE waited 1.85 us at c_f2:1. Theory P (moving the gate's middle steps by 0.7 us lets c_gate:7 start beside GpSimd's b_kv and wait it out): c_gate:7 takes 1.8 us again, 2440 to 2470 us. Rival (b_s:5's move did it): c_gate:7 stays at 0.4 to 0.5 us, time at most 2401 us, 2381 if the gap at b_s:5 goes for good.

Measured: 2450.91 us, 1.0211 (1.0188 to 1.0234), by theory P. `c_gate:7` (L903, two instructions), GpSimd beside it and TensorE's `c_f2:1`:

```profile
1638.39 1.84 DVE L903 SCALAR_TENSOR_TENSOR g_mask<-constants,g_idx_f,g_mask 128x8 f32<-128x8 f32 x2
1640.16 0.68 DVE L928 SCALAR_TENSOR_TENSOR acc<-ps_c_out,x 128x512 f32<-128x512 f32 x1
```

```profile
1638.06 1.16 POOL L489 TENSOR_TENSOR ctxT_lo<-ctxT,ctxT_hi 128x512 f16<-128x512 f32 x1
1639.17 1.04 POOL L534 TENSOR_TENSOR c_hidden<-c_relu 128x512 f32<-128x512 f32 x1
```

```profile
1640.98 0.27 PE L965 MATMUL ps_c_out<-w_hi,c_hidden_hi 128*128 128x256 f16 x1 [1.85 <-DVE acc L928]
```

The pair starts 0.33 us behind L489 (the end of `b_kv`), waits it and then L534 out (until 1640.21), and ends at 1640.23. In e7 it starts 0.28 us before L486 ends and 0.36 us ahead of L489, and takes 0.44 us. That VectorE's step slips in or waits twice is a matter of some tenths of a microsecond.

> The kernel before, in which TensorE alone is changed: c_f2:2 stands right behind c_f2:1, ahead of a_pt:6, c_f1:5, b_s:7 and b_pv:3 (together 2.2 us). It asks for c_f2:2 as early as the new order does. If the loss in the new orders comes from the early place alone (rival T), the gap before c_f2:2 is 2.9 us (0.70 before), a second half-clock stretch comes with it, and the time is 2400 + 31 x (2.2 + 1.0) = 2500 us. Theory V (in the new orders VectorE's queue sets this stretch, so that the fill alone gave nothing) says for the old ones: VectorE's c_f2:1 ends at 26.3 us behind b_wo's start and is not the bound, so TensorE's gap is a full loss here too, 2470 to 2500. Under 2420 us: neither gap nor clock costs what they show.

```diff
     tensor (on the kernel before)
-        ... b_pv:2 c_f2:1 a_pt:6 c_f1:5 b_s:7 b_pv:3 c_f2:2 b_s:8 ...
+        ... b_pv:2 c_f2:1 c_f2:2 a_pt:6 c_f1:5 b_s:7 b_pv:3 b_s:8 ...
```

Measured: 2522.53 us, 1.0519 (1.0493 to 1.0546), 122 us or 3.9 us per interval, more than both theories gave. TensorE waits 2.84 us at `c_f2:2` in the interval below, as expected (2.9), and what I had left out comes behind it: VectorE waits 5.29 us for `b_s:7`'s scores and hands 0.77 us back to TensorE's `b_s:8`.

```profile
1682.38 0.27 PE L965 MATMUL ps_c_out<-w_hi,c_hidden_hi 128*128 128x256 f16 x1 [2.84 <-DVE acc L936]
...
1688.43 0.39 PE L1088 MATMUL ps_b_scores<-k_stack_even,q_stack 128*128 128x256 f16 x2 [0.77 <-DVE b_neg_max L828]
```

```profile
1687.59 0.42 DVE L828 CUSTOM_DVE_ANT_0 b_neg_scores<-ps_b_scores,bias 128x256 f32<-128x256 f32 x1 [5.29 <-PE ps_b_scores L1088]
```

The clock was 0.955, 113 us lost against 110: in this execution almost the whole loss is waiting (the other three were granted 0.948 to 0.950). Of its 31 gaps of 2.8 us at `c_f2:2` only 9 have a half-clock stretch behind them.

## Why the prediction was wrong

Per interval, with the waits of the lists above divided by 31:

| term | forecast | measured |
|---|---|---|
| (1) stack loads | -1.3 | -0.3 in the change (-9.7 us); -0.2 by earlier loads alone (e8) |
| (2) `b_wo` to `c_f2:2` | -0.5 | +1.5: `c_f2:2` +1.7 (acc), scores +1.1, `c_T` +0.6, c_relu -1.3, `a_pt` -0.6 |
| (3) behind `a_wo` | +0.9 | +0.5: `c_f2:6` +0.3 (the rest of acc), transposes +0.2 |
| clock | in (1), -0.2 | +0.8 (24 us) |
| sum | -0.9 | +2.5; by the spans +2.6, by the writes of x2 +2.9 |

**Term (1) was mis-sized by four to six times, and the reading behind it failed.** The prediction took a DMA share of 1.10 to 1.26 for traffic that could be moved out of the way. But the share counts the time that packets take, and it rises without more bytes. Two stretches of 18 us ahead of `b_s:0` in the kernel before, the second that of [rows 5] (the last two columns are DMA share and GB/s):

```profile
1564.02:1582.02 18.00, 18.00 (x228) 16.59 (x226) 17.44 (x65) 17.38 (x55) 15.89 (x15) 1.00 0.83 195
1917.90:1935.90 18.00, 15.24 (x198) 13.83 (x196) 15.05 (x56) 16.12 (x54) 15.02 (x17) 0.98 1.20 198
```

The first has no wait of `b_s:0`, the second one of 2.76 us, at the same bytes. Worked out so for 30 intervals of this trace, 12 have a share above 1.04: their packets take 54 ns in the mean, and `b_s:0` waits 1.94 us. In the other 18 packets take 36 ns and the wait is 0.49 us, at 190 GB/s against 180. After the change 13 of 30 are still of the slow kind, with two bias loads close ahead of the stack instead of three. So late stacks go with slow packets and not with more traffic; what makes packets slow is not on record. In quick intervals the issues are the likelier bound: `b_s:0` starts 2.3 us behind the last of them in the mean, against 4.3 in the slow kind. One quick interval, after the change: the 16 issues run from 1630.15 to 1639.63, 9.5 us, and `b_s:0` starts at 1641.62, 2.0 us behind the last and 0.84 us late, at a share of 0.74, though the last bias load had left at 1624.34:

```profile
1624.34 0.57 SPq L369 DMA_DIRECT2D bias<-in_bias  x1
...
1630.15 5.70 SPq L414 DMA_DIRECT2D q_stack<-qk_scratch  x8
...
1637.78 1.85 SPq L403 DMA_DIRECT2D k_stack_odd<-qk_scratch  x4
```

I had named the issues as the other bound (0) and took the value near 1.5 on the argument that the wait came in only 22 of 31 intervals. That an event comes at times speaks for a margin near zero, not for its size being curable. The rival "the loads don't matter" was nearly right in its size; its reason, the issues, fits the quick intervals alone.

**Term (2) holds the larger error. The step that failed is "then 0.5 before `b_s:6` and 1.1 before `c_f2:2`, which needs `c_f2:1` and so the gate's end".** The new gaps up to that point were about as forecast (`c_T`, `b_s:1` and `b_s:6` 1.03, 1.05 and 0.44 us, forecast 1.19, 1.39, 0.5), and the relief at `a_pt:4` and the c_relu waits came. It was smaller than forecast: the waits from `b_s:1` to ahead of `b_s:5` fell by 0.4 us per interval (83.8 to 72.9 us in all), some 0.7 with the overlap counted, not by 1.6. The prediction had read them from one undisturbed interval, where `a_pt:4` waits 0.89 us; the median of the 31 is 0.22. Then `c_f2:2` waited 2.40 us, not 1.1. The prediction follows `c_gate:4` to `c_gate:7` against GpSimd's stream and names no price for the last gate step, and that one fell on two GpSimd instructions and took 2.27 us, with the same two durations in 30 of the 32 batches, against 1.25 before. The gate's steps as a whole did not get dearer (their durations add up to 284 us before and 260 after); the one that got dearer is the one that `c_f2:1` waits for. With one of its two collisions gone the time falls by 40 us (e2). The rival of the gate chain (2410 to 2450 us) had the right mechanism at the wrong step: it watched `c_gate:5`, whose cast took 0.17 us after, and `b_s:5` lost only 0.50 us. Nearest came both rivals at once, 2469 us, which the range had left out.

**Two more things the walk had too small or left out.** It followed VectorE's lateness behind the gate to one waiter, `c_f2:2`. There was another, `b_p:4` in VectorE's queue and by it ScalarE, GpSimd and `c_f2:3`. The prediction had named `c_f2:3`, but with 0.3 us and by way of `b_p:5`; once `c_f2:2`'s gap is filled (e1), `c_f2:3` waits 0.81 us and `a_pv:5` 0.93 in the median. e1, e5 and e6 show that each way alone holds the whole loss, and that both must be opened. And it priced gaps at their length and their overlap, with no second fall of the clock: +24 us, and part of each later gain (e6, e9, e10).

**Term (3)** was of the right sign and half the size, but not at `a_q:0`, where the gap stayed (0.22 us before, 0.25 after, in the median).

**Is the early place of `c_f2:2` the cause by itself?** In the old orders it costs 3.9 us per interval (e15), in the new ones undoing it alone gives nothing (e1). Both are shown. The loss of the change is the product of TensorE's early ask and VectorE's late end, not of one of them. The three moves of e7 account for the whole 3.7%; which share of it belongs to each can't be given, since they don't add. Left open: why the packets are slow in some intervals, and what decides whether a gap brings a half-clock stretch.

## What to carry to other kernels

When a hand-written order is changed, list for the late engine all that stands behind the late step in its queue, and follow each to its reader: a fill in front of one waiter gives nothing (e1: 0 us) while the other is late (e6: 73 us with both). Small instructions of VectorE beside a stream of GpSimd's have no price of their own, theirs is 0.22 to 1.3 us by their start; look for a place in the order where GpSimd is idle anyway, and put the chain's last one there. Don't swap one engine's list alone to test it: e3 and e4 lost 230 and 286 us by that; move single steps.

## What the runs showed of the hardware that was not expected

- Two gate instructions in a row waited out two GpSimd instructions in a row (1661.46 to 1663.73, and 1638.39 to 1640.23): GpSimd's next instruction gets in between them, so a pair pays twice. After the change the last step's two took about 1.05 and 1.31 us in 30 of the 32 batches.
- The half clock depends on what stands ahead of it, but not on the length of one gap alone. Half-clock stretches behind the gap, in 31 intervals: 23 at a gap of 2.40 us (after), none at 1.31 us (e2), 9 at 1.85 us before `c_f2:1` (e14), 9 at 2.84 us in the old orders (e15). A filler of 0.5 us of matmuls ahead of `c_T` (e10) took 6 us of waiting away and 32 us of clock.
- A DMA share above 1 did not mean more bytes: 1.20 at 198 GB/s against 0.83 at 195, with packets of 54 against 36 ns in the mean of such intervals.
